# Attention after the weighing: normalised with pixels on partitions, turned back in two blocks, and its bias added by GpSimd

## The reference, cut to what matters

```
attn = jax.nn.softmax(jnp.einsum('bhqd,bhkd->bhqk', q, k) * scale, axis=-1)
out = jnp.einsum('bhqk,bhkd->bhqd', attn, v)
out = out.transpose(0, 2, 1, 3).reshape(b, n, c)
out = out @ proj_w + proj_b
return out.transpose(0, 2, 1).reshape(b, c, h, w) + x
```

## Time and profile before

| | |
|---|---|
| median of 3 runs | 13677.38 us (13676.63 to 13682.44) |
| profiled execution | 13678.15 us, span 13676.6 us |
| PE matmuls busy | 12133.8 us, 89% |
| DVE busy | 9880.2 us, 72% |
| ACT busy | 7245.6 us, 53% |
| POOL busy | 2772.1 us, 20% |
| L900, the reductions of the maxima (DVE) | 3225.8 us, 4096 of 818 ns |
| L695, the weighing (PE) | 1633.2 us, 12288 matmuls |
| L1202, the spread reciprocals (POOL) | 327.4 us, 512 of 639 ns |

### The profile page before, as it was taken

How to read it: one execution, slowest core, us unless ns; L and a number is a source line. 1 busy time by engine, 2 the same in 40 slices (tenths; PEclk the granted TensorE clock), 3 DMA queues, 4 the chain that set the end, 5 groups by cost and what they waited for, 6 DMA issues and landing times. The chain is left out here.

```text
span 13676.6 us, 211412 instructions
## 1 busy us (share of the span) xinstructions
PE 12133.8 (89%) x76449; PEld 6936.8 (51%) x76449; DVE 9880.2 (72%) x17164; ACT 7245.6 (53%) x12557; POOL 2772.1 (20%) x4024
## 2 busy tenths in 40 slices
PE   2999899998989889899998999989999898988989
PEld 1645546455454544546455464554645546454454
DVE  7867767776677767768677686776777667776776
ACT  4556455564546545455454555645556454664545
POOL 1210312113131131311203121031211313113131
PEclk9999899999989999899998999989999999999989
DMA  1021120202212021130211202112021120202112
GB/s 43 16 41 39 36 59 18 52 26 42 53 26 51 20 46 50 26 69 1 48 47 33 62 9 46 41 36 59 16 50 30 39 56 25 51 20 46 50 26 63
DMA packets 170752, 535.69 MB, mean 39 GB/s; under 512 B 70424, under 2 KB 86808, under 8 KB 154800
## 3 DMA queue, kind: packets, MB, share of 16 engines
q1 hardware_dynamic: 169648, 521.28, 16.8%
HBM read 235.78 MB, written 67.11 MB: 22 GB/s over the span
## 5 line engine op out<-in xcount | busy, mean ns | idle before, releaser
L900 DVE TENSOR_REDUCE R<-ps 128x2 f32<-128x640 f32 x4096 | 3225.8, 818 | 673.4 <-PE ps L649 657.0
L1096 ACT ACTIVATE R<-ps 128x512 f32<-128x512 f32 x5120 | 2830.0, 592 | 1272.5 <-PE ps L670 1261.7
L225 ACT ACTIVATE R<-R,st 128x1475 bf16<-128x1475 f32 x1326 | 2021.2, 1524 | 529.9 <-DVE st L301 434.9
L289 DVE TENSOR_SCALAR_CACHE_REDUCE R<-R,st 128x1255 bf16<-128x1255 f32 x1326 | 2009.9, 1516 | 17.1
L649 PE MATMUL ps<-KST,R 96*128 96x320 bf16 x8192 | 1882.4, 313 | 41.9 <-DVE R L900 26.0
L695 PE MATMUL ps<-R 128*32 128x512 f32 x12288 | 1633.2, 604 | 1.7
L670 PE MATMUL ps<-R,KST 104*128 104x512 bf16 x4096 | 1580.6, 389 | 10.7 <-ACT R L1096 8.8
L649 PEld LDWEIGHTS ps<-KST,R 96*128 96x128 bf16 x8192 | 792.2, 100 | 788.3 <-DVE R L900 204.2
L437 PE MATMUL ps<-Wk,cst 128*128 128x266 f32 x4096 | 1118.2, 397 | 0.0
L1202 POOL COPY R<-R 128x512 f32<-128x512 f32 x512 | 327.4, 639 | 3737.0 <-DVE R L933 3737.0
L241 POOL TENSOR_SCALAR st<-st 128x1 f32<-128x1 f32 x442 | 99.1, 224 | 4232.2 <-DVE st L296 4228.1
(11 more groups left out here) (188 smaller groups left out, 20217.0 us busy)
## 6 DMA issues: line engine op xcount, KB each, us to landing
R<-R SPq DMA_DIRECT2D x3072, 64.0 KB, 2.4
R<-xh_in SPq DMA_DIRECT2D x136, 512.0 KB, 4.5
out_dram<-Z SPq DMA_DIRECT2D x16, 4096.0 KB, 14.2
R<-xa_in SPq DMA_DIRECT2D x36, 1024.0 KB, 11.2
R<-xb_in SPq DMA_DIRECT2D x34, 1024.0 KB, 12.5
R<-sr_in SPq DMA_DIRECT2D x32, 1024.0 KB, 6.4
R<-Wk SPq DMA_DIRECT2D x2048, 8.0 KB
R<-sr_in SPq DMA_DIRECT2D x16, 2016.0 KB, 9.3
```

What stands on the lines that cost most here:

```text
L225: e.activation(junka[:, 0:o2 - o1], xc[:, o1:o2], ACT.Sign, bias=mid, scale=-1.0, accum_out=cnt[:, NP + i:NP + i + 1]).then_inc(md_ca, 1)
L289: e.tensor_scalar(junk[:, 0:o1 - o0], xc[:, o0:o1], mid, None, ALU.is_le, ALU.add, accum_out=cnt[:, i:i + 1]).then_inc(md_cv, 1)
L900: e.tensor_reduce(MX[(4 * u + s4) % 2][:, blk_, h0:h0 + 2], ps[:, 2 + 2 * bq:4 + 2 * bq, 0:320], axis=AX.X, op=ALU.max).then_inc(mx, 1)
L1096: e.activation(PB[:, t % 2, w, :], ps[:, w % 2, :], ACT.Exp).then_inc(ex, 1)
```

## The change

The product of a step is now normalised where its pixels are on partitions. `denominators` on DVE takes the reciprocal (now L931) and then multiplies the 16 channels of each of 4 x 4 heads, read from bank 6, by it (now L935); `ON` holds 256 elements of 64 packed channels for each of four blocks of pixels. POOL's spreading (`RX`) and the multiply of 512 elements are gone. `turn_back` on PE transposes two blocks of pixels at a time, so two transposes bring all back (L712 in the new kernel as well), ACT copies them to `OX`, and two matmuls with the weights twice on a diagonal project them (L719). The bias is added to `Z` by POOL, in `add_bias`: a quarter of the columns each time, once ahead of the attention loop and then once behind the fourth stage part of each group. The weighing rounds i = 0 and i = 1 both stand in round 2 now; they were in rounds 1 and 3.

```diff
 # DVE
 def denominators(t):
+    heads = ps[:, 6, :].rearrange("p (a d) -> p a d", a=16)
     e.wait_ge(den_ps, t + 1)
-    if t > 1:
-        e.wait_ge(rx, t - 1)
-    e.reciprocal(RD[t % 2], ps[:, 6, :].rearrange("p (a h d) -> p a h d", a=4, h=4)[:, :, :, 16]).then_inc(rc, 1)
-def normalise(t):
-    e.wait_ge(nt_ps, t + 1)
+    e.reciprocal(RD[t % 2], heads[:, :, 16]).then_inc(rc, 1)
     if t:
-        e.wait_ge(po_ps, t)
-    e.tensor_tensor(ON, OR[t % 2], ps[:, 6, :], ALU.mult).then_inc(nm, 1)
+        e.wait_ge(ot_ps, t)
+    e.wait_ge(rc, t + 1)
+    e.tensor_tensor(ON.rearrange("p (a d) -> p a d", a=16), heads[:, :, 0:16],
+                    RD[t % 2].unsqueeze(2).to_broadcast([128, 16, 16]), ALU.mult).then_inc(on, 1)
...
 def project_out(t):
-    zo_ = Z[:, :, w0:w0 + 7:2].rearrange("p c w -> p w c")
+    zo_ = Z[:, :, w0:w0 + 7:2]
     e.wait_ge(po_ps, t + 1)
+    if t % 8 == 0:
+        e.wait_ge(zb, t // 8 + 1)
-    e.tensor_tensor(zo_, ps[:, 6, :].rearrange("p (w c) -> p w c", w=4)[:, :, 0:64], zo_, ALU.add).then_inc(zo, 1)
+    e.tensor_tensor(zo_, ps[:, 6, 0:256].rearrange("p (w c) -> p c w", w=4), zo_, ALU.add).then_inc(zo, 1)
...
 # PE, in the loop over w
-if w == 1 and prev:
-    weigh(t - 1, 0)
 if w == 1 and t and t + AHEAD - 1 < NT:
     lay_max(t + AHEAD - 1)
-if w == 3 and prev:
+if w == 2 and prev:
+    weigh(t - 1, 0)
     weigh(t - 1, 1)
 if w == 3 and done2:
-    normalise(t - 2)
+    turn_back(t - 2)
...
 # ACT, in the loop over w
+if w == 3 and t >= 2:
+    e.wait_ge(ot_ps, t - 1)
+    if t > 2:
+        e.wait_ge(po_ps, t - 2)
+    e.activation(OX, ps[:, 6, 0:256], ACT.Copy).then_inc(ox, 1)
...
 # POOL
+def add_bias(g):
+    zg = Z[:, :, 32 * g:32 * g + 32]
+    if g == 0:
+        e.wait_ge(xf, 16)
+    e.tensor_tensor(zg, zg, c("pb").unsqueeze(2).to_broadcast([128, C, 32]), ALU.add).then_inc(zb, 1)
+
+add_bias(0)
...
-        if w == 9 and prev:
-            k = (t - 1) % 2
-            e.wait_ge(rc, t)
-            if t > 2:
-                e.wait_ge(nt_ps, t - 2)
-            if t == 1:
-                e.wait_ge(ka, 8)
-            e.tensor_copy(RX[k].rearrange("p (a h d) -> p a h d", a=4, h=4),
-                          RD[k].unsqueeze(3).to_broadcast([128, 4, 4, 32])).then_inc(rx, 1)
+        if w == 0 and live and u % 2 and s4 == 0 and u < 7:
+            add_bias(u // 2 + 1)
```

More of the change, by code:

```diff
@@ L132, in program @@
               for i in range(2)]
-        RD = [R2[:, 2640 + 16 * i:2656 + 16 * i].rearrange("p (a b) -> p a b", a=4) for i in range(2)]
-        RX = [R2[:, 512 * i:512 * i + 512] for i in range(2)]
+        RD = [R2[:, 2640 + 16 * i:2656 + 16 * i] for i in range(2)]
         MR = [W[0:8, 2560 + 256 * i:2816 + 256 * i].bitcast(BF16) for i in range(2)]
         OR = [W[:, 512 * i:512 * i + 512] for i in range(2)]
-        ON = W[:, 1024:1536]
+        ON = W[:, 1024:1280]
+        OX = W[:, 1280:1536]
         RS = [W[:, 1536 + 512 * i:2048 + 512 * i] for i in range(2)]
@@ L144, in program @@
          q_ps, qh, qr, qm, ql, c1_ps, c2_ps, kd, ka, kp, kg,
-         mx_ps, mx, m8, lay_ps, mr, sc_ps, ex, va_ps, vm, vx, pv_ps, ou, den_ps, rc, rx, nt_ps, nm, po_ps, zo,
+         mx_ps, mx, m8, lay_ps, mr, sc_ps, ex, va_ps, vm, vx, pv_ps, ou, den_ps, rc, on, ot_ps, ox, zb, po_ps, zo,
          in_w1, in_dr, in_xc0, in_xc1, in_w20, in_w21, in_w22, in_qs0, in_qs1, in_qs2, in_m0, in_m1,
@@ L705, in denominators, with turn_back @@
                 op.then_inc(den_ps, 1)
-                b6[0] = (rc, t + 1)
-            def normalise(t):
-                e.wait_ge(rx, t + 1)
+                b6[0] = (on, t + 1)
+            def turn_back(t):
+                e.wait_ge(on, t + 1)
                 e.wait_ge(*b6[0])
[L711 to L714, removed]
+                for i in range(2):
+                    op = e.transpose(ps[:, 6, 128 * i:128 * i + 128], ON[:, 128 * i:128 * i + 128], c("ident"))
+                op.then_inc(ot_ps, 1)
+                b6[0] = (ox, t + 1)
             def project_out(t):
-                e.wait_ge(nm, t + 1)
-                for i in range(4):
-                    op = e.matmul(ps[:, 6, 128 * i:128 * i + 128], lhsT=ON[:, 128 * i:128 * i + 128], rhs=c("pw"),
+                e.wait_ge(ox, t + 1)
+                for i in range(2):
+                    op = e.matmul(ps[:, 6, 128 * i:128 * i + 128], lhsT=OX[:, 128 * i:128 * i + 128], rhs=c("pw"),
                                   start=True, stop=True)
@@ L962, in vector @@
                         maxima(ahead // 4, ahead % 4, w)
-                    if w == 3 and done2:
-                        normalise(t - 2)
                     if w == 5 and done2:
@@ L1101, in scalar @@
                         if t > 2:
-                            e.wait_ge(nm, t - 2)
+                            e.wait_ge(den_ps, t - 2)
                         e.activation(OR[(t - 1) % 2], ps[:, 7, :], ACT.Copy).then_inc(ou, 1)
@@ L1398, in host_layout @@
     pw = np.zeros((128, 128), np.float32)
-    for h in range(4):
-        pw[32 * h:32 * h + 16, 0:64] = g["proj_w"][16 * h:16 * h + 16]
-    pw[16, 0:64] = g["proj_b"]
+    for k in range(2):
+        pw[64 * k:64 * k + 64, 64 * k:64 * k + 64] = g["proj_w"]
     put("pw", pw)
+    put("pb", np.tile(g["proj_b"], (128, 1)))
     def taps(w, k):
```

## The result

| | median us | lowest to highest | ratio to before, 95% interval |
|---|---|---|---|
| before (4 runs) | 13678.11 | 13676.63 to 13682.44 | |
| changed kernel (4 runs) | 14030.41 | 14013.34 to 14035.23 | 1.0255 [1.0237, 1.0273] |

The forecast was 13900, slower; the measured time lies in the range, 10 us under the upper end of the likeliest case's own (14040): +352 us where +222 was forecast.

The account below looks back on a forecast made before the run. PE was taken as the bound, provided nothing makes it wait. Per image -4.3 plain, +3.7 stage, +9.6 bias, +4.5 clock, +3.8 median, -3.4 ends gave +13.9 us, times 16 images +222: 13900 us, range 13560 to 14050.

Parts of the forecast that it names:

- likeliest case: Whole kernel, all terms as worked out: slower, 13780 to 14040 us; chance 0.55.
- GpSimd's lock: Three steps an image: GpSimd's bias addition holds DVE's split, taken at 3.74 us; +9.6 us an image.
- Rival 2: GpSimd's additions do not hold DVE beyond what is seen now: faster, 13565 us; chance 0.13.
- Half clock: PE at 1.2 GHz behind the idle of three bias steps, 1.5 us each: +4.5 us an image.
- Plain steps: Attention steps: PE saves 0.8 us but waits 0.4 in round 2; 0.27 less a step, -4.3 an image.
- Rival 3: The lock is there, but PE's round 2 is not held in plain steps: 13690 us, no change; chance 0.10.
- Steps with a stage: Six steps an image with a q stage in round 0: 0.6 us more each, +3.7 an image.
- The median's additions: GpSimd's additions, no longer paced, run in steps 24 to 27 and hold DVE's split: +3.8 us an image.
- rival 5: Worse: DVE's multiply takes 0.70 us and the holds by the median also halve the clock: 14110 us; chance 0.12.
- Ends: Steps 30 and 31 and the two behind: chain shorter by 1.2 us a pass, about -3.4 an image.

Follow-up runs that it names:

- e2: Changed kernel with only the bias additions in the loop held back until DVE has split the step's maxima: 13800.41 us, ratio 1.0087.
- e4: Changed kernel with each bias addition cut into four instructions of 512 elements, at the same place in the queue: 13918.95 us, ratio 1.0173.
- e7: Changed kernel with DVE splitting the maxima right behind round 7's reduction, GpSimd and weighing left as they were: 13715.06 us, ratio 1.0031.
- e5: Changed kernel with bias and median additions both held until the split, and weighing rounds back in rounds 1 and 3: 13312.52 us, ratio 0.9731.
- e10: Changed kernel with only the weighing rounds back in rounds 1 and 3, GpSimd's additions left unpaced: 13724.15 us, ratio 1.0032.
- e1: Changed kernel with only GpSimd's median additions held back until DVE has split the maxima: 14000.85 us, ratio 1.0233.
- e3: Changed kernel with both the median and the bias additions held back until DVE has split the maxima: 13758.17 us, ratio 1.0058.
- e6: Kernel before the change with nothing but its two weighing rounds adjoined in round 2: 13951.84 us, ratio 1.02.
- e8: Changed kernel with both GpSimd additions paced, the split behind round 7's reduction, weighing back in rounds 1 and 3: 13327.97 us, ratio 0.9743.
- e9: Changed kernel with both GpSimd additions paced and the split behind round 7's reduction, weighing rounds still adjoined: 13558.33 us, ratio 0.9914.

## Why the prediction was right, and where its sizes were off

**GpSimd's lock (right).** The prediction took the upper end, 3.74, for L910's hold, from two rows with holds of 0.84 at most. It is 3.56 (L909 now). Round 2's L649 stands at S + 5.89 where 5.85 was worked out, and PE idles for 3.83 where 3.9 was. Rival 2, that nothing beyond the seen holds happens, is refuted by the row itself and by e2, e4 and e7: the same addition is harmless when DVE does not go from SBUF to SBUF beside it, and a shorter instruction gives a shorter hold. The Trainium skill (SBUF — State Buffer, "SBUF: two separate sides") has the shared ports locked for a whole instruction; by that rule the forecast was made at 3.74, and the trace agrees with 3.56 of 3.63.

**Half clock (right, too low).** Hold and clock together were forecast as 3 x 3.2 + 3 x 1.5 = 14.1 us an image and came to 15.2. The hold is as forecast, 3.2 net a step, and the steps grew by 5.1 on average, so the clock takes about 1.9 instead of 1.5 (an estimate: the difference of the two). e4 shows the clock's part apart: 14.06 against 11.37, 2.7. The bound of "3.4 us at half speed" was too short: it lasts 5 us from PE's restart in the first image. For the same hold the images differ, with 16.4 to 16.6 or 15.4 in step 3, depending on when the clock fell.

**Plain steps (right in kind, -0.18 instead of -0.27).** The hold came where it was said, through the multiply (0.425, forecast 0.43) and the reduction, at S + 1.20 instead of S + 1.14: what stands behind the multiply is later by 0.50 and not by 0.45. L649 ran at S + 2.07 instead of S + 2.00 and round 3 began at S + 4.30 instead of S + 4.21; the 6.00 from there to the next step are as worked out. So the missing 0.09 lies ahead of round 3. L657's wait of 0.19 for the split, which was not in the prediction, does not add to it. Rival 3, that the hold does not show, is refuted: e5 with 9.75 shows what that would look like. The Trainium skill (TensorEngine Tiling (Array Packing), "Key Properties") has PE drain at each change of the tiling mode, which spoke for adjoining. By the rows the gain is at most 2 x 1.06 - 1.92 = 0.2 a step, it was in the sum as 0.1, and the measurement goes against adjoining: 0.55 more a step with the late split (10.30 against 9.75), 0.25 with the early one.

**Steps with a stage (right in kind, +5.3 instead of +3.7).** The prediction's own 0.43 and 8.75 less 8.52 make 0.66 a step and 4.0 an image, not 3.7. Four of the steps took 0.66 to 0.77 more; t = 1 and t = 2 took 1.1 and 1.3. Step 2 is 14.05 in 11 images and 16.43 in the five in which half clock falls into it, which makes up 0.7 of its 1.3. The prediction had no clock term here.

**The median's additions (right in kind, +5.2 instead of +3.8).** Steps 25 and 27 at +2.8 instead of three at +1.4. Where the additions fall was off: they began 0.7 and 1.0 ahead of D and not 0.3, so the first one was over when the split began, and the cast was held by the second alone (1.70 and 1.35), in two steps and not in three and a half. That each step then cost twice the forecast is the clock: behind PE's 1.72 of waiting half clock follows (the weighing of 3.24 above), which is the second half of rival 5. That the total came out near is luck, fewer holds at a higher price; e10 shows the holds as the prediction had them, one addition for each instruction of the split, and there they cost 7.7. e1 takes all of it back. The other half of rival 5, a multiply of 0.70, is refuted.

**Ends (right).** -3.4 forecast, -3.3 measured. The first bias addition costs nothing, as said (t = 0: -0.02).

**Not in the sum.** +0.9 us an image outside the loop. Most of it is the clock: of the 15 stretches between loops nine are short (476) and six long (479 to 480), before it was twelve and three (479), and short ones differ by 0.2 to 0.5 us between the two kernels. This term was 0 in the forecast; it is 5.3 in e1 and 4.6 in e3, and with such a one the changed kernel would have been at some 14090 to 14100 (an estimate), outside the range. That it stayed inside is luck to this extent.

Together: the profiled span grew by 335.5 us (14012.1 less 13676.6), 113 more than the 222 of the sum. Of these some 33 are in the plain steps, 25 in those with a stage, 22 in the median's, 17 in those with the bias and 14 outside (differences per image by 16); the remaining 2 are the ends and rounding. All of them lie on the same side, so no term made good for another. The other 17 of the 130 that the medians miss are the distance of this one execution from its kernel's median.

What is shown: the lock as the cause of the long steps (e1, e2, e4, e7, e10 against e5), the adjoined rounds as a cost of their own in both kernels (e6, e8 against e9), and that the new chain by itself is a gain (e5). What stays open: why the clock falls where it does, outside the loop and in step 2. That it moves without an edit there is shown; no run was made to place it.

## What to carry to other kernels

A long GpSimd instruction costs nothing where DVE's instructions beside it read PSUM, and holds one that goes from SBUF to SBUF to its end: look at what DVE does from SBUF to SBUF at that time and who waits for it, and let GpSimd wait until that is over. Here one wait in each of two places was worth 412 us (272 with the adjoined rounds), and without them the better chain looked like no gain. Second, before matmuls are gathered in one place to save changes of mode, ask what latency they covered where they were: to save 0.1 a step cost 0.55 net.

## What the hardware showed that was not expected

- The same 2440 matmuls ahead of the attention loop took 448.7 or 457.5 us in one execution, with a granted clock of 0.94 and 0.92, though no instruction in them had changed. For e1 and e3 such stretches add up to 75 to 85 us of 13700.
- Half clock lasted some 5 us from PE's restart behind an idle of 3.8 us, so that the standing cost half as much again as it took itself (1.9 on average, an estimate).
- The granted clock fell without any such idle too: in image 2 of the changed kernel it is 0.50 for 6.8 us from 1.2 us into step 2, and the longest idle of PE in steps 0 to 2 ahead of it is 1.30 us. The same step with the same waits keeps full clock in 11 of the 16 images.
- When GpSimd had several instructions queued, DVE got in between two of them with one instruction: L907 was held to the end of one and L909, a moment later, to the end of the next (0.43 and 3.56 in the bias step, 0.43 and 0.99 with the pieces of e4).
- The addition into Z out of PSUM fell from 0.696 to 0.415 when the same 256 elements were walked in another order and read from one row instead of four pieces. Which of the two did it no run separates.
